# Denominator sums of four key tiles in eleven quarters of the second batch, ordered by due time, and one side piece a block in turns 13 and 14

## The reference, cut to what matters

```python
q = (x1 @ wq.T)   # (b, 16 heads, 1024, 32)
k = (x2 @ wk.T); v = (x2 @ wv.T)   # (b, 16 heads, 2048, 32)
dots = einsum('bhnd,bhmd->bhnm', q, k) * SCALE
attn = softmax(dots, axis=-1)
out = einsum('bhnm,bhmd->bhnd', attn, v)
```

## Time and profile before

| what | us |
|---|---|
| median of three runs | 1981.41 (1978.61 to 1984.81) |
| the profiled execution's own time | 1983.6 |
| its span in the trace | 1981.9 |
| mean granted TensorE clock | 0.98 |

### The profile page before, as it was taken

How to read it: one execution, slowest core, us unless ns; L and a number is a source line. 1 busy time by engine, 2 the same in 40 slices (tenths; PEclk the granted TensorE clock), 3 DMA queues, 4 the chain that set the end, 5 groups by cost and what they waited for, 6 DMA issues and landing times.

```text
span 1981.9 us, 26338 instructions
## 1 busy us (share of the span) xinstructions
PE 1894.3 (96%) x9904; PEld 1261.1 (64%) x9904; DVE 1218.2 (61%) x2279; ACT 884.2 (45%) x1587; POOL 817.0 (41%) x735
## 2 busy tenths in 40 slices
PE   8999999989999999999999999999969999999992
PEld 6876665667655555555445545544449999888991
DVE  6565553247678788888678778778544444444433
ACT  3212322312466666666456456456624443333431
POOL 3002201100288788888567567565022222332112
PEclk9999999989999999999999999999969999999996
DMA  7003523574668476757444434421253445454316
GB/s 272 22 1 112 186 85 138 193 206 134 157 134 185 97 180 139 168 122 157 94 112 97 103 85 109 107 62 63 75 176 91 125 131 139 104 141 111 96 18 190
DMA packets 123694, 243.53 MB, mean 123 GB/s; under 512 B 11152, under 2 KB 29344, under 8 KB 119520
## 3 DMA queue, kind: packets, MB, share of 16 engines
q1 hardware_dynamic: 108608, 185.46, 31.8%
q0 software_dynamic: 13872, 54.30, 13.8%
q10 hardware_dynamic: 1088, 2.10, 0.3%
HBM read 147.15 MB, written 62.42 MB: 106 GB/s over the span
## 4 chain that ended last, share of the span: by engine, by line
PE 83%; DVE 12%; DMA 2%; issue 1%; ACT 1%; SPq 1%; POOL 0%; ACTq 0%; POOLq 0%; DVEq 0%
PE banks L1122 36%; PE banks L1384 12%; PE banks L1291 11%; PE banks L1261 10%; PE banks L1280 8%; DVE max L1562 8%; PE banks L1312 4%; PE banks L1128 2%; DMA raw<-in_x_t 1%; DMA k_parts<-out_lo 1%; DVE stats_y L1770 0%; PE banks L1199 0%; DVE src_lo L1428 0%; DVE den_c L1581 0%; ACT src_hi L1817 0%
## 5 line engine op out<-in xcount | busy, mean ns | idle before, releaser
L1562 DVE TENSOR_REDUCE max<-banks 128x1 f32<-128x512 f32 x1024 | 627.7, 682 | 140.9 <-PE banks L1261 140.1
L2033 POOL TENSOR_TENSOR probs<-probs,probs 128x512 f32<-128x512 f32 x464 | 582.9, 1290 | 246.2 <-PE banks L1291 246.2
L1913 ACT ACTIVATE probs<-banks 128x512 f32<-128x512 f32 x1024 | 520.2, 607 | 257.7 <-PE banks L1280 257.1
L1261 PE MATMUL banks<-k_stack,q_stack 98*128 98x512 f32 x1024 | 428.7, 426 | 4.1 <-DVE max L1562 2.8
L1280 PE MATMUL banks<-q_stack,k_stack 98*128 98x512 f32 x1024 | 376.8, 398 | 2.6 <-ACT probs L1913 2.6
L1261 PEld LDWEIGHTS banks<-k_stack,q_stack 98*128 98x128 f32 x1024 | 192.1, 188 | 194.4 <-DVE max L1562 106.5
L1291 PE MATMUL banks<-probs,v_grp 128*32 128x512 f32 x2048 | 250.2, 601 | 0.0
L1280 PEld LDWEIGHTS banks<-q_stack,k_stack 98*128 98x128 f32 x1024 | 191.6, 188 | 61.7 <-ACT probs L1913 17.9
L2080 POOL DMA_INDIRECT y_rows<-eo,tok x40 | 79.8, 1996 | 216.2 <-DVE eo L1763 170.4
L1750 DVE TENSOR_TENSOR hid_lo<-hid,hid_hi 128x640 fp32r<-128x640 f32 x64 | 52.9, 826 | 143.1 <-ACT hid_hi L1978 143.1
L2044 POOL TENSOR_TENSOR x_nat<-x_nat,bxo_row 128x512 f32<-128x512 f32 x16 | 21.1, 1351 | 262.7 <-PE banks L1128 262.7
(11 more groups left out here) (228 smaller groups left out, 2696.8 us busy)
## 6 DMA issues: line engine op xcount, KB each, us to landing
k_stack<-k_parts SPq DMA_DIRECT2D x144, 256.0 KB, 5.2
w_raw<-in_L_ffn_w SPq DMA_DIRECT2D x16, 2048.0 KB, 8.3
probs<-probs POOLq DMA_DIRECT2D x31, 1024.0 KB, 10.3
q_stack<-q_parts SPq DMA_DIRECT2D x48, 256.0 KB
v_grp<-v_rows SPq DMA_DIRECT2D x48, 256.0 KB, 3.3
raw<-in_ctx_t SPq DMA_DIRECT2D x8, 1024.0 KB, 6.5
k_parts<-out_hi SPq DMA_DIRECT2D x32, 256.0 KB, 2.5
k_parts<-out_lo SPq DMA_DIRECT2D x32, 256.0 KB, 2.9
```

What stands on the lines that cost most here:

```text
L1261: nc.tensor.matmul(out, queries_of(t)[:, j, tile_of(k)], keys_of(t)[0:STK + SHIFT, j, mc * HALF:(mc + 1) * HALF], start=True, stop=True) \
L1562: V.reduce_max(max4[:, tiles_of(t), :, :][:, k, j, mc:mc + 1], bank(bank_of["max", t, mc, k, j]), AX.X) \
L1913: S.activation(probs_of(t, s)[:, j, :], bank(bank_of["score", t, s, j]), ACT.Exp, scale=SCALE) \
L2033: G.tensor_tensor(a[:, j, :], a[:, j, :], b[:, j, :], ALU.add).then_inc(pair_added.sem, 1)
```

## The change

It names eleven quarters of turns 8 to 13 in which `by_fours` also holds: quarters 0, 1, 2 of turn 8, 2 of turn 9, 1 and 2 of turn 10, 0 and 2 of turn 11, and 0, 1, 2 of turn 13. Their pair sums are added by the transfer of L2037, and one den stands for two. The entry of quarter 2 of turns 7 to 15 is due three blocks after its close instead of four. `pending` is sorted by due time before its head is looked at, so that a pair no longer stands behind a four that is due later, and the first den of a turn, whichever it is, takes the bank and starts its sum (`den_begun`). Last, a block of turn 13 or 14 runs no piece with PE behind a piece without PE; only turn 15 does.

```diff
+LAST_BEFORE_PLAIN = {(t, 2) for t in range(2 * NG - 1, 4 * NG)}
+
+LATER_FOURS = {(8, 0), (8, 1), (8, 2), (9, 2), (10, 1), (10, 2), (11, 0), (11, 2), (13, 0), (13, 1), (13, 2)}
...
         def by_fours(t, s):
-            return t * MT + s < B * NG * MT - FOUR
+            return t * MT + s < B * NG * MT - FOUR or (t, s // FOUR) in LATER_FOURS
...
         def denominators(until):
+            pending.sort(key=lambda due: due[0])
             while pending and pending[0][0] <= until:
                 _, t, s = pending.pop(0)
-                if s == (3 if by_fours(t, 0) else 1):
+                if t not in den_begun:
                     take_bank(("den", t), DEN)
+                    den_begun[t] = s
                 do("den", t, s)
...
-                if not busy or turn >= LAST - 2:
+                if not busy or turn == LAST:
                     side(WITH_PE)
...
                     elif s % FOUR == 2:
                         fours.append((turn, s + 1))
-                        pending.append((clock + 4, turn, s + 1))
+                        pending.append((clock + (3 if (turn, s // FOUR) in LAST_BEFORE_PLAIN else 4), turn, s + 1))
...
             def denominators_of(t, s):
-                begun = s == (3 if by_fours(t, 0) else 1)
+                begun = s == den_begun[t]
```

More of the change, by code:

```diff
@@ L764, in side @@
             return True
-        divisions, pending, later, fours, divisions_from = [], [], [], [], [0]
+        divisions, pending, later, fours, divisions_from, den_begun = [], [], [], [], [0], {}
         clock = 0
```

## The result

The changed kernel takes 1992.09 us in the median of five runs (1989.76 to 1994.44), against 1982.35 for the kernel before in its five. The ratio is 1.0047, with a 95% interval of 1.0035 to 1.006. I had forecast 8.5 us less.

What follows compares the result with a forecast made beforehand. PE, busy 96% of the span, was taken as the bound. Terms -9.5 - 0.9 + 3.5 - 0.4 - 1.2 = -8.5 us took the median from 1981.4 to 1972.9, range 1968 to 1979.5.

Steps and rivals of the forecast that it cites:

- cover: POOL's added issues of 0.87 us and later additions cost nothing, since 1.4 us lie before the den that reads them.
- What DVE gives back: Blocks losing their only den have 1.08 us of DVE slack; DVE's delays beyond it cost +3.5 us, bounds 0 and 5.
- Dens, -9.5: Eleven quarters of turns 8 to 13 lose one den each on PE, at 0.86 us: -9.5 us.
- Block 65's wait, -0.9: In block 65 a den no longer waits behind ACT's copy of the bank: -0.9 us.
- ACT, -0.4: Block 111's second den moves block 112 back but not ACT's activations, so its exponentials start less late: -0.4 us.
- Side pieces, -1.2: Block 114 loses 2.34 us, block 115 gets `ranks`, +0.63, and DVE's delay, +0.5: -1.2 us, bounds -2 to +1.
- The slower rival: Fours land too late for their dens in five tight quarters, at 20 us: +10.2 us, 1991.6; chance 0.07.
- The clock has nothing to give: In both batches of cross attention PE's granted clock is 1.00, so no gain comes from it.
- The signs of being wrong: PE waits for a four's transfer; POOL's adds reach PE late; or 79, 91 and 111 are no longer than plain blocks.

Runs made afterwards that it cites:

- e5: The kernel before with the dens of four pairs cut to eight columns of one head and no transfer added; ratio 1.0009 to the kernel before.
- e7: The kernel before with a piece without PE run after a block's sixth maximum instead of the fifth; ratio 1.0022 to the kernel before.
- e2: The changed kernel without the later quarters (8, 2), (9, 2), (11, 0) and (11, 2), seven staying; ratio 0.9954 to the kernel before.
- e10: The changed kernel with eight later quarters, chosen so each block ahead of a routing chain has a den: e8 without (12, 2); ratio 0.9935 to the kernel before.
- e6: The kernel before with the changed rule for side pieces alone; ratio 0.9981 to the kernel before.
- e8: The changed kernel with nine later quarters, (12, 2) among them, chosen so each block ahead of a routing chain has a den; ratio 0.9948 to the kernel before.
- e11: The changed kernel without the later quarter (11, 0) alone; ratio 0.9978 to the kernel before.

## Why the prediction was wrong

**The forecast's sign and its range are wrong.** The step that failed is the one on cover: "its adds end about 4.4 behind the next block's start, and the den that reads them comes at about 5.8, so 1.4 us cover it". The times are right (4.41 in blocks without a den ahead, 5.84 in block 59), and nothing waits longer for the sums than before (weight loads 0.5 us once, in either kernel). But I looked only for who reads POOL's additions, not for what else their presence stops. With it fell the paragraph "What DVE gives back": it let each DVE operation keep its length and only added up the work against 6.50. In block 90 I had the maxima start 1.41 late in block 91; one operation took 5.23 instead of 0.17.

The Trainium skill (SBUF — State Buffer, "Who interferes with whom") says that DVE and GpSimd share a pair of SBUF ports, that a DVE instruction with two SBUF inputs contends with a GpSimd instruction that reads SBUF, that one in a 2-port mode contends with GpSimd too, and that the later one is blocked until the other ends. The trace agrees in what is held: 5.23 instead of 0.17 for L1540, and in e5 1.17 for `rt_chosen`, which takes 0.21 in e7, where it begins behind POOL's work. It goes beyond the page in how long: L1540 is on record 0.02 us ahead of the first of the four additions that it outlasts. That POOL's additions hold these operations is shown by the runs; that the ports do it, and that L1540, with its one input, ran in such a mode, no run here shows. I had not weighed it.

The kernel before had shown the hold. In blocks 72, 74, 79, 90 and 111 one operation takes 0.2 to 0.3 us more than its like. In block 90 it is this first row, which I had in view and read as a slow first operation: 0.46 instead of 0.16, until a division of POOL's has ended, the second row.

```profile
1166.50 0.46 DVE L1530 TENSOR_SCALAR rsqrt_a<-mean_var 128x4 f32<-128x4 f32 x1
...
1166.46 0.48 POOL L2060 TENSOR_TENSOR heads_t<-num_c,den_c 128x128 f32<-128x128 f32 x1
```

Much plainer is block 116, behind the last maxima, where L1697 takes 1.25 beside three of POOL's additions. In block 79 it takes 0.23:

```profile
1370.12 1.25 DVE L1697 TENSOR_TENSOR rt_picked<-rt_chosen,rt_sv 128x64 f32<-128x64 f32 x1
1371.40 0.22 DVE L1699 TENSOR_REDUCE slot<-rt_picked 128x8 f32<-128x64 f32 x1
...
1368.75 3.78 POOL L2033 TENSOR_TENSOR probs<-probs,probs 128x512 f32<-128x512 f32 x3
```

Point by point:

- *Dens, -9.5.* Right. A den is 0.86 as only one, as second, and removed: 5.95 in 83 and 84, 7.68 in 64, 11.47 in 87. e2 and e10 rest on it and come out as worked out.
- *Block 65's wait, -0.9.* Right: 5.96.
- *What DVE gives back, +3.5.* Right where the chains met little of POOL: 110 and 111 (5.96 and 8.44), 66 and 105 (0.2 to 0.3 for 0.28). Wrong where they did, in 71, 79, 90 and 95, each behind a block without a den: 14.9 us more, with what followed. I had put 70 and 89 at nothing.
- *ACT, -0.4.* Wrong and small. Block 112's exponentials do start 0.78 behind the block instead of 1.18, as I had it, but the block took 8.84, 0.87 over before. In e10 they start 1.18 behind, and it takes 8.83: the late start had cost nothing.
- *Side pieces, -1.2.* Right: 6.82 and 7.91, and alone in e6.
- *The slower rival.* It had the sign, and its 1991.6 lies 0.5 from the measured 1992.09, by luck; its mechanism is not the one: in the changed kernel fours land in 10.2 us in the median and 14.0 at most, and no row shows PE waiting for one. It is real 1 us deep in e8's (12, 2), where 13.9 us are left and the four lands in 14.9.
- *The clock.* "The clock has nothing to give" was true of before only. After the stops of PE the granted clock is 0.82, 0.67 and 0.82 in blocks 72, 91 and 96. PE had stood 2.1, 5.9 and 1.8 us in blocks 71, 90 and 95. By blocks, 4.1 of the 14.9 us lie in 72, 91 and 96, where the clock fell. The other 10.7 lie in 71, 78 to 80, 90, 92 and 95, at a granted clock of 0.98 to 1.00, and so are waiting. e11 shows 91 without a fall: 7.30.
- *The signs of being wrong.* None of the three came: PE never waits at L1318 for a transfer, the additions reach it no later, and 79, 91 and 111 are longer than a plain block. They tested the cover and the sums, not the lengths of DVE's operations.

## What to carry to other kernels

When PE's work in a loop is cut, list what every other engine does at each moment of the period, not only who waits for whom: a shorter period moves them against each other, and POOL can hold DVE without a semaphore between them. The chance of seeing it beforehand is in single rows of the kind "same operation, several times its usual length". Where the loop has short gaps that a chain just fits in, remove work from periods that are not followed by a chain. Here eight removals so placed gained more than eleven, and even work on constants, put back in seven blocks, gained 11.4 us on the changed kernel.

## What was unexpected of the hardware

- A held DVE operation does not always get in after one POOL instruction. In blocks 71 and 95 each waits for one addition, the first of block 71 also for the division behind it (1.1 to 1.35 us). In block 90 one waits for four additions in a row (5.23 us). What decides was not tried. It is not the order of the two starts alone: L1540 begins 0.02 us ahead of the additions in both blocks, and takes 5.23 us in 90 and 0.17 in 71.
- Not every DVE operation is stopped. A reduction within SBUF, L1699 in block 116 above, takes its 0.22 beside an addition. The reciprocals of `den_c` (L1587) and the maxima from PSUM keep their lengths beside POOL's additions too, as in block 79 of the changed kernel:

```profile
1067.51 0.54 DVE L1587 RECIPROCAL den_c<-den_c 128x64 f32<-128x64 f32 x1
1067.97 3.01 DVE L1568 TENSOR_REDUCE max<-banks 128x1 f32<-128x512 f32 x5
1072.74 1.28 DVE L1710 COPY before<-before 128x8 f32<-128x8 f32 x1
...
1065.75 5.28 POOL L2039 TENSOR_TENSOR probs<-probs,probs 128x512 f32<-128x512 f32 x4
1072.71 3.74 POOL L2039 TENSOR_TENSOR probs<-probs,probs 128x512 f32<-128x512 f32 x3 [1.28 <-PE banks L1297]
```

A copy of eight columns, at 1072.74, takes 1.28 us with the additions that begin at 1072.71. In the kernel before the same copy takes 0.17.
